# Graph attention layer on one core: transposes moved ahead of the next scores, four PSUM banks for them, normalised attention in SBUF

## What is computed

```python
q = (x @ Wq.T); k = (x @ Wk.T); v = (x @ Wv.T + bv)          # split into 12 heads
scores = einsum('bqhd,bkhd->bhqk', q, k) * scale + (adj + adj)
scores = where(any(scores != 0, axis=-1), scores, -inf)      # a row that is all zero gives no attention
p = nan_to_num(softmax(scores, axis=-1))
out = einsum('bhqk,bkhd->bqhd', p, v).reshape(b, n, h)
x = layernorm(x + out @ Wo.T + bo)
```

## Time and profile before

| what | value |
| --- | --- |
| median of 3 runs | 620.27 us (620.02 to 621.94) |
| the profiled execution, its own time | 619.91 us |
| span of its profile | 617.7 us |
| PE busy | 606.6 us (98%) |
| ACT / DVE / POOL busy | 503.3 / 477.6 / 410.5 us |
| TensorE clock granted, mean over the span | 0.998 |

### The profile page before, as it was taken

One profiled execution on the slowest core, in us unless ns is written; L12 is line 12 of the kernel. 1 busy time (PEld: TensorE's weight loads), 2 busy tenths in 40 slices (PEclk: granted clock), 3 DMA queues, 4 the chain that ended last, 5 costly groups with the idle time before them and its releaser, 6 DMA issues.

```text
span 617.7 us, 22924 instructions
## 1 busy us (share of the span) xinstructions
PE 606.6 (98%) x8250; PEld 503.2 (81%) x8250; DVE 477.6 (77%) x2376; ACT 503.3 (81%) x1944; POOL 410.5 (66%) x499
## 2 busy tenths in 40 slices
PE   9999999999999999999999999999999999999996
PEld 5788888888888888888888888888888888888774
DVE  4677877877877877877877877877877877877886
ACT  4788878879788788878879788788878879778893
POOL 0676767767667676767767667676767767656663
PEclk9999999999999999999999999999999999999999
DMA  9410423222242321434222242421423221222111
GB/s 300 152 38 22 135 90 129 86 75 88 83 141 83 125 84 37 134 90 129 87 79 85 82 140 79 136 81 36 131 89 129 87 78 37 79 89 84 54 53 52
DMA packets 33424, 58.51 MB, mean 95 GB/s; under 512 B 9888, under 2 KB 22688, under 8 KB 33312
## 3 DMA queue, kind: packets, MB, share of 16 engines
q1 hardware_dynamic: 32880, 56.47, 28.6%
q10 hardware_dynamic: 432, 0.59, 0.3%
HBM read 43.52 MB, written 13.53 MB: 92 GB/s over the span
## 4 chain that ended last, share of the span: by engine, by line
PE 91%; DVE 4%; issue 1%; POOLq 0%; ACT 0%; DVEq 0%; POOL 0%
PE qk_ps L343 34%; PE vo_ps L375 15%; PE vo_ps L431 15%; PE scores_ps L360 9%; PE scores_ps L388 8%; PE att_ps L411 8%; DVE nscores L577 2%; PE qk_ps L431 2%; DVE stats L661 1%; DVE y L658 1%; DVE att_t L649 0%; DVE att_ps L607 0%; PE qk_ps L329 0%; DVE recip L613 0%; DVE probs_t L592 0%
## 5 line engine op out<-in xcount | busy, mean ns | idle before, releaser
L483 ACT ACTIVATE probs<-nscores,neg_max 128x128 f32<-128x128 f32 x768 | 298.1, 394 | 85.2 <-DVE neg_max L577 85.2
L577 DVE CUSTOM_DVE_ANT_0 nscores<-scores_ps,adj_n 128x128 f32<-128x128 f32 x768 | 167.3, 287 | 23.6 <-PE scores_ps L360 22.3
L292 POOL TENSOR_TENSOR tree<-nscores 128x768 f32<-128x768 f32 x64 | 120.2, 1878 | 59.4 <-DVE neg_max L577 58.0
L483 ACT ACTIVATION_READ_ACCUMULATOR probs<-nscores,neg_max 128x1 f32 x768 | 147.4, 192 | 0.0
L375 PE MATMUL vo_ps<-w_v,x_t 128*128 128x384 f32 x576 | 111.8, 338 | 0.0
L274 POOL TENSOR_TENSOR x_t<-x_raw,x_t 128x512 fp32r<-128x512 f32 x45 | 59.0, 1314 | 79.2 <-ACT x_t L500 79.2
L292 POOL TENSOR_TENSOR tree<-tree 128x384 f32<-128x384 f32 (+1 forms) x128 | 103.9, 812 | 10.0
L343 PE MATMUL qk_ps<-x_t,w_q 128*128 128x512 f32 x405 | 110.6, 411 | 0.0
L343 PE MATMUL qk_ps<-x_t,w_k 128*128 128x512 f32 x405 | 110.4, 411 | 0.0
L375 PEld LDWEIGHTS vo_ps<-w_v,x_t 128*128 128x128 f32 x576 | 102.4, 188 | 6.0
L431 PE MATMUL vo_ps<-w_o,att_t 128*128 128x384 f32 x522 | 101.6, 339 | 0.0
(11 more groups left out here) (71 smaller groups left out, 681.3 us busy)
## 6 DMA issues: line engine op xcount, KB each, us to landing
x_n<-xn SPq DMA_DIRECT2D x32, 384.0 KB, 5.4
out<-out_n SPq DMA_DIRECT2D x31, 384.0 KB, 5.0
x_raw<-xt SPq DMA_DIRECT2D x15, 768.0 KB, 6.5
scale_t<-scale_mem SPq DMA_DIRECT2D x58, 192.0 KB
adj_n<-adj SPq DMA_DIRECT2D x32, 128.0 KB, 4.5
scale_mem<-scale_rows SPq DMA_DIRECT2D x58, 16.0 KB
x_raw<-xt SPq DMA_DIRECT2D x3, 256.0 KB, 5.3
nscores<-wq ACTq DMA_DIRECT2D x3, 192.0 KB, 4.0
```

Of the source, the lines that this page charges most:

```text
L292: nc.gpsimd.tensor_tensor(tree[:, b % 2, :, 0:width], src[:, :, 0:width], src[:, :, width:2 * width], ALU.add).then_inc(tree_step, 1)
L483: last = nc.scalar.activation(probs[:, b % 2, h], nscores[:, b % 2, h], ACT.Exp, bias=neg_max[:, b % 2, h:h + 1], scale=-1.0, accum_out=ro ...
L577: last = nc.vector.tensor_tensor_reduce(out=nscores[:, half, h], in0=scores_ps[j][:, m * P:(m + 1) * P], in1=adj_n[:, b // 2 % 2, half], s ...
```

## The change

- TensorE's iteration becomes: `turn(b)`, `score(b+1)`, first projection tile, `values(b+1)`, second tile (odd iterations only), `project_out(b-1)`, `attend(b)`. Tiles are no longer split: two in an odd iteration, one in an even one. The matmuls on zeros of the last iterations are gone.
- The transposes have banks of their own: `qk_ps[0]`, `v_ps`, `qk_ps[1]`, `spare_ps`. The same banks take the first tile, the values and the second tile, each of which waits for the copy of the transposes out of its bank.
- The output projection goes to `scores_ps[0]`, the attention to `scores_ps[1]`. So `score(b+1)` waits for `y_ready` of b-2 and for `att_done` of b-1, and `project_out(b-1)` and `attend(b)` wait for all of `biased` of b+1.
- `normalise` writes `att_n` in SBUF, from which `attention_high` and `attention_low` read; `total` and `nonzero` are in SBUF too.
- ScalarE copies three of the four transposed banks in every iteration, VectorE one. VectorE copies the first projection tile (`keep_first`), ScalarE the second (`keep_second`).
- VectorE's iteration begins with `normalise(b-1)` and `find_scale(b)`. The tree of sums is made in two parts, of 8 and 4 heads.
- Only the last batch takes the direct way for its scale.

The core of the diff:

```diff
+PARTS = ((0, 2 * HPT), (2 * HPT, HEADS))
+STEPS = TREE * len(PARTS)
+LOWS = 3
+        turn_ps = [qk_ps[0], v_ps, qk_ps[1], spare_ps]
+        att_ps = scores_ps[1]
         def out_bank(b):
-            return qk_ps[b % 2] if ending(b + 1) else vo_ps
+            return scores_ps[0] if has(b + 1) else scores_ps[2]
         def projected(b):
-            if b < -1 or ending(b):
-                return (), ()
+            if not -1 <= b < NB - GRP - 1:
+                return ()
             tile = (b + 1) // 2 * 3
-            if b % 2 == 1:
-                return ((tile, 0, FULL),), ((tile + 1, 0, PART),)
-            return ((tile + 1, PART, FULL), (tile + 2, 0, PART)), ((tile + 2, PART, FULL),)
+            return (tile, tile + 1) if b % 2 == 1 else (tile + 2,)
...
+            def project(b, n, tile):
+                if b >= 0:
+                    pe.wait_ge(turned_low, LOWS * b + (1, 3)[n])
...
             def score(b):
                 wait(pe, biased, KT * b)
+                wait(pe, y_ready, b - 2)
+                wait(pe, att_done, b - 1)
...
             def values(b):
-                if b < 3 or ending(b - 2):
-                    wait(pe, v_ready, b)
-                else:
-                    pe.wait_ge(y_ready, b - 2)
+                if b > 0:
+                    pe.wait_ge(turned_low, LOWS * (b - 1) + 2)
...
             def turn(b):
-                pe.wait_ge(biased, KT * (min(b + 1, NB - 1) + 1))
+                pe.wait_ge(kept_first, firsts(b - 1))
+                pe.wait_ge(kept_second, seconds(b - 1))
+                pe.wait_ge(v_ready, b + 1)
...
+            def free_scores(b):
+                pe.wait_ge(biased, KT * min(b + 1, NB))
             def attend(b):
+                free_scores(b + 1)
...
             def project_out(b):
-                free_out_bank(b)
+                free_scores(b + 2)
+                wait(pe, y_ready, b)
...
             for b in range(-1, NB + 1):          # TensorE
-                ahead, behind = projected(b)
+                if has(b):
+                    turn(b)
                 if has(b + 1):
                     score(b + 1)
+                for n, tile in enumerate(projected(b)):
+                    project(b, n, tile)
+                    if n == 0:
+                        values(b + 1)
+                if has(b + 1) and not projected(b):
                     values(b + 1)
+                if has(b - 1):
+                    project_out(b - 1)
                 if has(b):
                     attend(b)
...
             for b in range(-1, NB + 2):          # ScalarE
+                if has(b - 1):
                     attention_high(b - 1)
                 if has(b):
                     keep_turned_low(b)
                 if has(b + 1):
+                    for m in range(KT):
+                        softmax_top(b + 1, m)
+                if len(projected(b)) > 1:
+                    keep_second(b)
...
             for b in range(-1, NB + 1):          # VectorE
+                if has(b - 1):
                     normalise(b - 1)
                 if has(b):
                     find_scale(b)
+                if has(b + 1):
+                    bias_and_max(b + 1, 0)
+                    bias_and_max(b + 1, 1)
                 if has(b - 1):
                     attention_low(b - 1)
+                if has(b + 1):
+                    bias_and_max(b + 1, 2)
+                if has(b):
                     keep_turned_high(b)
+                if projected(b):
+                    keep_first(b)
+                if has(b + 1):
+                    keep_v(b + 1)
+                    if has(b - 1):
+                        residual(b - 1)
```

More of the change, by code:

```diff
@@ L68, in build @@
         tree = sb("tree", [P, 2, HEADS, P // 2])
+        total = sb("total", [P, HEADS])
+        nonzero = sb("nonzero", [P, HEADS])
         recip = sb("recip", [P, HEADS])
@@ L158, in wait @@
                 eng.wait_ge(semaphore, value)
[L160 to L162 removed]
         def direct(b):
[L166 to L169 removed]
+            return b == NB - 1
         def columns(b):
@@ L283, in sum_scores @@
             def sum_scores(b):
-                pool.wait_ge(biased, KT * (b + 1))
                 wait(pool, total_done, b - 1)
[L287 to L294, removed]
+                for part, (low, high) in enumerate(PARTS):
+                    pool.wait_ge(biased, KT * b + high // HPT)
+                    src = nscores[:, b % 2, low:high]
+                    for n in range(TREE):
+                        width = P >> (n + 1)
+                        if n:
+                            pool.wait_ge(tree_step, b * STEPS + part * TREE + n)
+                        nc.gpsimd.tensor_tensor(tree[:, b % 2, low:high, 0:width], src[:, :, 0:width],
+                                                src[:, :, width:2 * width], ALU.add).then_inc(tree_step, 1)
+                        src = tree[:, b % 2, low:high]
             def find_rstd(b):
@@ L329, in run_idle @@
                     nc.tensor.matmul(bank[:], zeros[:, 0:P], zeros[:], start=True, stop=True)
-            def project(tile, first, end):
+            def project(b, n, tile):
                 g, t = tile // TILES + 1, tile % TILES
                 w, cols = (w_k, w_q)[t // KT], slice(t % KT * P, (t % KT + 1) * P)
[L335 to L341, removed]
-                        pe.wait_ge(x_split, KT * (g - 1) + k + 1)
[L343 to L346, removed]
+                if b >= 0:
+                    pe.wait_ge(turned_low, LOWS * b + (1, 3)[n])
+                elif n:
+                    pe.wait_ge(first_keys, KT)
+                for k in range(KT):
+                    if t == 0:
+                        pe.wait_ge(x_split, KT * (g - 1) + k + 1)
+                    for i, (a, c) in enumerate(TERMS):
+                        last = nc.tensor.matmul(qk_ps[n][:], w[:, a, k, cols], x_t[:, g % XBUFS, c, k],
+                                                start=(k == 0 and i == 0),
+                                                stop=(k == KT - 1 and i == len(TERMS) - 1))
+                last.then_inc(proj_done, 1)
             def score(b):
```

165 lines of the change are left out of this document (53 added, 112 removed).

## The result

The changed kernel takes 638.98 us (median of 4 runs, 638.83 to 640.06), the kernel before 620.14 us beside it (619.51 to 621.94): ratio 1.0303, 95% interval 1.0278 to 1.0327. It is slower by 18.8 us; the forecast was 632.0 us, with 621 to 650 as its range. The profiled execution took 640.06 us, its span is 638.3 us, 20.6 more than the 617.7 of before. It is the longest of the four: the spans of the others are 637.0 to 637.2 us, so 1.1 to 1.3 of the 20.6 us belong to this one execution.

What follows compares the result with a forecast made beforehand. The kernel was taken to be bound by TensorE's own work until b = 58. The forecast was 619.91 + 11.6 (29 pairs at 0.40) + 1.8 (start) - 1 (end) = 632.3, say 632 us, range 621 to 650.

Steps and rivals of the forecast that it cites:

- the likeliest case: Steady iterations: every pair 0.16 to 0.57 us longer, with TensorE waiting for the normalisation; 625 to 637 us; chance 0.60.
- Part 2: Scores wait for `att_done`: a chain of 1.89 us against 1.58 of cover, so TensorE waits 0.31 us in every iteration.
- Part 1: TensorE's own work: without any wait the pair of iterations takes 18.04 to 18.13 us, 0.37 to 0.46 gained.
- Part 3: First tile waits for ScalarE's first copy of the transposes: nothing to 0.16 us, taken as 0.10.
- The start: Before the scores of batch 2: they start near 36.4 instead of 34.56 us, +1.8, with the second tile made whole.
- The end: Ending iterations: 8.0 us against 8.05; with the last batches' shorter ways -1 us in all (0 to -2).
- The sum: Whole kernel: 619.91 + 11.6 for the pairs + 1.8 at the start - 1 at the end = 632.3 us.
- Rival B: GpSimd holds VectorE instructions with two SBUF operands, `find_scale` losing some 0.9 us per even iteration; 648 us; chance 0.20.
- Rival C: At the scores' start TensorE never waits for the normalisation, the chain being 1.58 us; faster, 608.5 us; chance 0.12.
- Rival D: Within 0.3%: the waits come out at their lower bounds and the end gains 2 us; +2 or less; chance 0.08.

Runs made afterwards that it cites:

- Experiment 1: Changed kernel with a second statistics instruction on the residual, its result unused: 656.66 us, ratio to the kernel before 1.057.
- experiment 2: Changed kernel with the attention normalised in place in PSUM, so the next scores also wait for `attention_low`: 771.15 us in one run.
- experiment 3: Changed kernel with VectorE's statistics of the residual of b-2 moved behind `normalise(b-1)`: 644.75 us; with `total` and `nonzero` also in PSUM 638.73 us.
- experiment 8: Changed kernel with matmuls on zeros around the second scores and in the ending iterations: 639.06 us, ratio 1.0308.
- experiment 6: Kernel before with `total`, `nonzero` and normalised attention in SBUF: 807.77 us; attention alone 656.38 us; `total` and `nonzero` alone 790.74 us.
- Experiment 5: Changed kernel with only `total` and `nonzero` put in unused columns of the spare PSUM bank: 638.01 us, ratio 1.0295.
- experiment 4: Changed kernel with residual statistics behind the next batch's bias, normalised output one iteration later: 677.28 us; with `total` and `nonzero` also in PSUM 646.44 us.

## Why the prediction was right, and where not

- **Direction and range** held, by the mechanism of the likeliest case: a wait once per iteration for the normalisation. The time lies 2 us above that case's own 625 to 637.
- **Part 2** forecast 1.89 us against a cover of 1.58, a wait of 0.31. Measured from rows: 315.72 - (312.67 + 1.73) = 1.32 from the projection's end to the normalisation, 0.54 for that, 0.14 to the scores, 2.00 in all; the attention and the transposes cover 1.66 of it (316.40 - 0.34 - 314.40), and the wait is 0.34. Experiment 1 shows that the chain counts one to one, and experiment 2 where the clock stays up. The release was taken too short (0.04, measured 0.14).
- **Part 1** said 0.37 to 0.46 saved. Without its waits the new pair is 18.89 - 0.68 = 18.21, so it is 0.29: from the first transpose to the scores 0.95 pass (305.93 - 0.34 - 304.64), where the earlier trace rows had 0.86 for them ahead of a projection.
- **Part 3** took 0.10 for a wait at the first tile; there is none. This and the release cancel, so the pair came out at +0.39 where +0.40 was said. The agreement to 0.01 is luck; the bounds, 0.16 to 0.57, are what the working supports.
- **The start** is the term that failed most: +1.8 forecast, +6.9 measured in the profiled execution. The second tile came as forecast (batch 1's scores 2.7 later). What the forecast lacked: the clock, 2.8; the wait of 1.15 for `normalise(0)`; and the 0.5 ahead of batch 0, which is not the change's; some 0.6 stay open. I followed the second tile and the transposes and not `find_scale(0)`, which now comes behind the whole tree with no earlier batch to hide it, and whose way over DRAM I had cost at nothing with "6 us or more" to spare. In the first batches that cover does not exist, and in steady state it is about 0.2 us in a one-tile iteration: experiment 3 took the statistics out of the chain, 0.5 us per iteration, and the normalisation waited for the scale.
- **The end**: -1 forecast, +2.8 measured. "I take it to stay at its upper level" did not hold, here and at the start; but experiment 8 had the clock up for most of the last 20 us and ended no sooner, so what the lower clock cost at the end is not shown. Batches 58 to 62 now fetch their scale over DRAM, where the kernel before took the direct way from batch 58 on (not 59, as written in the part on the kernel before: its page counts 58 transfers of `scale_t`, the new one's 63); by TensorE's waits that cost 0.9 us in two iterations. The rest stays open.
- **The sum** by measured terms: 28 pairs of 0.39 = 10.9, start 6.9, end 2.8: 20.6, against 12.4. The misses lie outside the pairs.
- **Rival B** (0.20) had the mechanism right and its price too low: a hold costs up to 1.1 us in the changed kernel and 1.5 in experiment 6, not 0.9. It comes once in four iterations and not in every second. It did not decide here, by the reason given against it: the holds fall where VectorE has a tile's time to spare, and `attention_low` (319.12) starts 0.24 ahead of the tree (319.36). Experiment 5 shows that next to nothing of the 18.8 us is due to it in the pairs (0.7 us from batch 4 to 58); experiments 4 and 6 what it costs where it is in a chain.
- **Rival C** asked for a chain of 1.58 us. Experiment 3 made it shorter by a statistics step, and the loop over DRAM took over. My forecast for it, 608.5, left that loop out: C could not have come true by that way.
- **Rival D** needed waits at the lower bounds and an end of -2; neither came.

## What to carry to other kernels

When a buffer gets a new owner, add up the chain that frees it and set it against the work that stands ahead of its next user: that gave the wait of the steady iteration to 0.03 us here. Then do the same once more for the first batches and the last ones, where nothing earlier hides a transfer and where TensorE pauses and its clock fell; here they held nearly half of the loss. And before a small VectorE operand moves from PSUM to SBUF, look which GpSimd instruction runs at that moment: the cost is the rest of that instruction, whatever the operand's size.

## What the runs showed that I had not expected

- Two tensors of 12 columns, moved from PSUM to SBUF in the kernel before, cost 171 us in 620 (experiment 6): 1.5 and 0.7 us of hold per iteration, and 2.7 us per iteration with the lower clock behind them.
- TensorE's clock fell to its lower level with pauses of 1.5 to 1.8 us in each iteration (experiments 2 and 6, both small steps: mean 0.90 and 0.93 from 100 to 600 us), though not behind every pause: in experiment 2 iterations of 9.52 and 11.60 us kept the upper level. With pauses of 0.34 it stayed there.
- The way of a 16 KB row scale to DRAM and back took 6.5 us at the end of the kernel (1.92 for the write, 4.53 for the read, which spreads it to 192 KB), three quarters of an iteration.
- A second, equal statistics instruction added 0.32 us, not its 0.56 us.
